# Layer norm's fp16 halves: the high half from one ScalarE instruction, the fp32 value and the low half on VectorE

## The reference

```
h = maximum(layernorm(x), 0);  x = x + attention(h, adj)     # 8 heads of 64, softmax over adj's edges
h = maximum(layernorm(x), 0);  x = x + relation(h, adj)      # rel = adj.T * (q k^T), each row divided by its norm; rel @ v
```

## Time and profile before

| what | value |
|---|---|
| median of 3 runs | 2466.06 us (2464.73 to 2466.9) |
| the profiled execution's own time | 2466.99 us |
| its span in the trace | 2465.2 us |
| TensorE busy, VectorE, ScalarE, GpSimd | 97%, 57%, 68%, 53% of the span |
| mean granted TensorE clock | 0.994 |

### The profile page before, as it was taken

The page is one execution under the profiler, slowest core; times in us unless marked ns, Lnnn a source line. Parts: engine busy times, 40 slices in busy tenths (PEclk is TensorE's granted clock), DMA queues, the critical chain, the costliest instruction groups (busy, mean ns, idle before and its releaser), DMA issues.

```text
span 2465.2 us, 53413 instructions
## 1 busy us (share of the span) xinstructions
PE 2396.9 (97%) x19252; PEld 1304.5 (53%) x19252; DVE 1411.2 (57%) x4432; ACT 1682.6 (68%) x4108; POOL 1296.1 (53%) x1159
## 2 busy tenths in 40 slices
PE   5899999999999999999999999999999999999986
PEld 2455555555555555555555555555555555555543
DVE  4555665555665555665555666555666555665543
ACT  4676766677766776766767766777766776766762
POOL 2555555555555555555555555555555555555541
PEclk9999999999999999999999999999999999999998
DMA  6566665775666666765666765666666666665642
GB/s 179 121 125 129 150 134 126 136 142 129 147 137 124 135 146 126 149 136 120 139 138 133 146 140 120 140 139 132 150 138 119 140 141 130 151 134 119 125 112 64
DMA packets 938792, 329.13 MB, mean 134 GB/s; under 512 B 885920, under 2 KB 886176, under 8 KB 938528
## 3 DMA queue, kind: packets, MB, share of 16 engines
q1 hardware_dynamic: 936272, 323.35, 63.1%
q10 hardware_dynamic: 2256, 2.36, 0.4%
HBM read 73.93 MB, written 33.55 MB: 44 GB/s over the span
## 4 chain that ended last, share of the span: by engine, by line
PE 89%; DMA 4%; ACT 3%; POOL 1%; DVE 1%; issue 1%; SPq 1%; DVEq 0%; ACTq 0%; POOLq 0%
PE B L677 75%; PE O L677 7%; PE S L751 7%; DMA probs_t<-halves 2%; DMA h0t<-h_halves 1%; ACT h L414 1%; ACT probs L474 1%; POOL h_halves L361 1%; PE B L707 1%; ACT h_halves L421 1%; POOL halves L375 1%; SPq L319 0%; POOL guess L356 0%; DMA h1t<-h_halves 0%; DVE masked L611 0%
## 5 line engine op out<-in xcount | busy, mean ns | idle before, releaser
L375 POOL TENSOR_TENSOR halves<-probs,halves 128x512 f16<-128x512 f32 x512 | 593.2, 1163 | 573.5 <-ACT halves L482 573.4
L474 ACT ACTIVATE probs<-masked,neg_max 128x256 f32<-128x256 f32 x1024 | 508.0, 497 | 229.6 <-DVE neg_max L611 229.5
L611 DVE CUSTOM_DVE_ANT_0 masked<-S,mask 128x256 f32<-128x256 f32 x1024 | 384.6, 418 | 126.4 <-PE S L751 126.3
L677 PE MATMUL B<-h0t,wq 128*128 128x512 f16 x1536 | 356.4, 382 | 32.2 <-DMA h0t<-h_halves 31.5
L361 POOL TENSOR_TENSOR h_halves<-h,h_halves 128x512 f16<-128x512 f32 x256 | 295.4, 1160 | 164.2 <-ACT h_halves L421 164.0
L677 PE MATMUL B<-wvt,h1t 128*128 128x512 f16 x1536 | 349.6, 381 | 9.8 <-DMA h1t<-h_halves 9.8
L677 PE MATMUL B<-h0t,wk 128*128 128x512 f16 x1536 | 352.8, 379 | 0.0
L677 PE MATMUL B<-wv,h0t 128*128 128x512 f16 x1536 | 352.2, 379 | 0.0
L677 PE MATMUL B<-h1t,wm 128*128 128x512 f16 x1536 | 346.9, 379 | 0.0
L482 ACT ACTIVATE halves<-probs 128x512 f16<-128x512 f32 x512 | 322.5, 630 | 16.2
L677 PEld LDWEIGHTS O<-v,probs_t 128*128 128x128 f16 x6144 | 248.3, 98 | 130.2 <-DMA probs_t<-halves 11.5
(11 more groups left out here) (70 smaller groups left out, 2894.7 us busy)
## 6 DMA issues: line engine op xcount, KB each, us to landing
x_in<-in_x_dram SPq DMA_DIRECT2D x128, 256.0 KB, 3.4
x_res<-in_x_dram SPq DMA_DIRECT2D x128, 256.0 KB, 3.7
out_dram<-result SPq DMA_DIRECT2D x128, 256.0 KB, 2.5
probs_t<-halves SPq DMA_TRANSPOSE x512, 2.8
h0t<-h_halves SPq DMA_TRANSPOSE x128, 3.2
h1t<-h_halves SPq DMA_TRANSPOSE x128, 3.3
rv<-in_L_gnn_Wq_dram SPq DMA_DIRECT2D x1, 1024.0 KB, 8.3
rq<-in_L_gnn_Wk_dram ACTq DMA_DIRECT2D x1, 1024.0 KB, 5.3
```

What stands on the lines that cost most here:

```text
L375: nc.gpsimd.tensor_tensor(halves[:, n % RING, 1, :], probs[:, n % 2, :, :].rearrange("p t n -> p (t n)"), halves[:, n % RING, 0, :], ALU.s ...
L474: ins = nc.scalar.activation(probs[:, n % 2, i, :], masked[:, n % 2, i, :], ACT.Exp, bias=neg_max[:, n % 2, i:i + 1], scale=-1.0, accum_ou ...
L611: ins = nc.vector.tensor_tensor_reduce(out=masked[:, n % 2, i, :], in0=S[n % 4][:, i, :], in1=mask[:, i, :], scale=SCORE, scalar=BIG, op0= ...
L677: ins = nc.tensor.matmul(dst, left(i), right(j), start=(n == 0), stop=(n == len(pairs) - 1))
```

## The change

In ln_apply's place ACT writes the fp16 high half directly, as relu(x * rstd + shift) rounded to fp16. DVE gets two instructions for each tile: `ln_apply`, a tensor_scalar that writes x * rstd + shift in fp32 to h (no ReLU), and `h_low_half`, a scalar_tensor_tensor that writes max(h, 0) minus the high half. POOL takes no part in either. A new step "low" in the plan says where DVE does the low half, and SP waits for and issues the transpose: for layer 1 within slot 12, for layer 0 in slots 18, 19, 22 and 25. The x loads now wait for the low half.

```diff
@@ BESIDE
-              12: [("ln1_scale", 0, 1), ("ln1_apply", 0, 1), ("ln1_split", 0, 1), ("ln1_apply", 1, 1),
-                   ("ln1_split", 1, 1), ("ln1_apply", 2, 1), ("ln1_split", 2, 1), ("ln1_apply", 3, 1),
-                   ("ln1_split", 3, 1), ("ln0_stats", 0, -1), ("ln0_stats", 1, -1)],
+              12: [("ln1_scale", 0, 1), ("ln1_apply", 0, 1), ("ln1_split", 0, 1), ("ln1_apply", 1, 1),
+                   ("ln1_split", 1, 1), ("ln1_low", 0, 1), ("ln1_apply", 2, 1), ("ln1_split", 2, 1),
+                   ("ln1_low", 1, 1), ("ln1_apply", 3, 1), ("ln1_split", 3, 1), ("ln1_low", 2, 1),
+                   ("ln0_stats", 0, -1), ("ln1_low", 3, 1), ("ln0_stats", 1, -1)],
...
-              18: [("ln0_apply", 0, -1), ("ln0_split", 0, -1), ("ln0_apply", 1, -1), ("ln0_split", 1, -1)],
+              18: [("ln0_apply", 0, -1), ("ln0_split", 0, -1), ("ln0_apply", 1, -1), ("ln0_split", 1, -1),
+                   ("ln0_low", 0, -1)],
+              19: [("ln0_low", 1, -1)],
               21: [("ln0_apply", 2, -1), ("ln0_split", 2, -1)],
+              22: [("ln0_low", 2, -1)],
               23: [("residual", 1, 0)],
-              24: [("ln0_apply", 3, -1), ("ln0_split", 3, -1)]}
+              24: [("ln0_apply", 3, -1), ("ln0_split", 3, -1)],
+              25: [("ln0_low", 3, -1)]}
@@ SP
-                    sp.wait_ge(ln_done[0], TILES * (p - 1) + n + 1)
+                    sp.wait_ge(h_low[0], TILES * (p - 1) + n + 1)
-                elif kind == "ln0_split" and p > 0:
+                elif kind == "ln0_low" and p > 0:
-                elif kind == "ln1_split":
+                elif kind == "ln1_low":
@@ POOL
-            def h_low_half(layer, n, pair):
-                pool.wait_ge(h_high[layer], TILES * pair + n + 1)
-                nc.gpsimd.tensor_tensor(h_halves[:, n, 1, :], h[:, n % 2, :],
-                                        h_halves[:, n, 0, :], ALU.subtract).then_inc(h_low[layer], 1)
@@ ACT
-                nc.scalar.activation(h[:, n % 2, :], src[:, n, :], ACT.Relu, scale=rstd[:, layer, n:n + 1],
-                                     bias=shift[:, layer, n:n + 1]).then_inc(ln_done[layer], 1)
-                nc.scalar.activation(h_halves[:, n, 0, :], h[:, n % 2, :],
-                                     ACT.Copy).then_inc(h_high[layer], 1)
+                nc.scalar.activation(h_halves[:, n, 0, :], src[:, n, :], ACT.Relu, scale=rstd[:, layer, n:n + 1],
+                                     bias=shift[:, layer, n:n + 1]).then_inc(h_high[layer], 1)
@@ DVE
+            def ln_apply(layer, src, n, pair, before, count):
+                dve.wait_ge(ln_scale[layer], pair + 1)
+                if n >= 2:
+                    dve.wait_ge(h_low[layer], TILES * pair + n - 1)
+                else:
+                    need(dve, before, count)
+                nc.vector.tensor_scalar(h[:, n % 2, :], src[:, n, :], rstd[:, layer, n:n + 1],
+                                        shift[:, layer, n:n + 1], ALU.mult, ALU.add).then_inc(ln_done[layer], 1)
+            def h_low_half(layer, n, pair):
+                dve.wait_ge(ln_done[layer], TILES * pair + n + 1)
+                dve.wait_ge(h_high[layer], TILES * pair + n + 1)
+                nc.vector.scalar_tensor_tensor(h_halves[:, n, 1, :], h[:, n % 2, :], 0.0, h_halves[:, n, 0, :],
+                                               ALU.max, ALU.subtract).then_inc(h_low[layer], 1)
```

More of the change, by code:

```diff
@@ L357, in ln_power @@
                                         ALU.pow).then_inc(ln_guess[layer], 1)
-            def h_low_half(layer, n, pair):
-                pool.wait_ge(h_high[layer], TILES * pair + n + 1)
-                nc.gpsimd.tensor_tensor(h_halves[:, n, 1, :], h[:, n % 2, :],
-                                        h_halves[:, n, 0, :], ALU.subtract).then_inc(h_low[layer], 1)
             ln_power(0, 1)
-            for n in range(TILES):
-                h_low_half(0, n, 0)
             for kind, n, p in pairs(PLAN):
@@ L381, in _ @@
                     ln_power(1, p + 1)
[L382 to L385, removed]
                 elif kind == "residual":
@@ L405, in _, with h_high_half @@
             act.dma_start(bv[:, :], bv0.partition_broadcast(P)).then_inc(small_loaded, 16)
-            def ln_apply(layer, src, n, pair, before, count):
+            def h_high_half(layer, src, n, pair, before, count):
                 act.wait_ge(ln_scale[layer], pair + 1)
[L410 to L413, removed]
-                nc.scalar.activation(h[:, n % 2, :], src[:, n, :], ACT.Relu, scale=rstd[:, layer, n:n + 1],
-                                     bias=shift[:, layer, n:n + 1]).then_inc(ln_done[layer], 1)
-            def h_high_half(layer, n, pair, before, count):
-                act.wait_ge(ln_done[layer], TILES * pair + n + 1)
                 need(act, before, count)
-                nc.scalar.activation(h_halves[:, n, 0, :], h[:, n % 2, :],
-                                     ACT.Copy).then_inc(h_high[layer], 1)
+                nc.scalar.activation(h_halves[:, n, 0, :], src[:, n, :], ACT.Relu, scale=rstd[:, layer, n:n + 1],
+                                     bias=shift[:, layer, n:n + 1]).then_inc(h_high[layer], 1)
             def weight_high(n, w, scale):
@@ L428, in _ @@
             for n in range(2):
-                ln_apply(0, x_in, n, 0, h_low[0], 0)
-            for n in range(2):
-                h_high_half(0, n, 0, h_turned[0][n], 0)
+                h_high_half(0, x_in, n, 0, h_turned[0][n], 0)
             act.dma_start(stage[1], wk0.rearrange("(t p) n -> p t n", p=P)).then_inc(w_loaded[1], 16)
@@ L434, in _ @@
             for n in range(2, 4):
-                ln_apply(0, x_in, n, 0, h_low[0], 0)
-            for n in range(2, 4):
-                h_high_half(0, n, 0, h_turned[0][n], 0)
+                h_high_half(0, x_in, n, 0, h_turned[0][n], 0)
             act.dma_start(stage[2], wv0.rearrange("(t p) n -> p t n", p=P)).then_inc(w_loaded[2], 16)
@@ L507, in _ @@
                     ins.then_inc(rel_high, 1)
-                elif kind == "ln0_apply" and p > 0:
-                    ln_apply(0, x_in, n, p, h_low[p > 1], TILES * max(p - 2, 0) + n + 3)
                 elif kind == "ln0_split" and p > 0:
-                    h_high_half(0, n, p, h_turned[p > 1][n], 16 * max(p - 1, 1))
-                elif kind == "ln1_apply":
-                    ln_apply(1, x_res[:, p % 2, :, :], n, p, h_low[0], TILES * min(p + 1, PAIRS - 1) + n + 3)
+                    h_high_half(0, x_in, n, p, h_turned[p > 1][n], 16 * max(p - 1, 1))
                 elif kind == "ln1_split":
-                    h_high_half(1, n, p, h_turned[0][n], 16 * min(p + 2, PAIRS))
+                    h_high_half(1, x_res[:, p % 2, :, :], n, p, h_turned[0][n], 16 * min(p + 2, PAIRS))
         @block.vector
@@ L563, in _ @@
             ln_scales(0, 1)
+            for n in range(2):
+                ln_apply(0, x_in, n, 0, h_low[0], 0)
+            for n in range(2):
+                h_low_half(0, n, 0)
             for n, (w, scale) in enumerate(((wq, QS), (wk, WS), (wv, WS))):
@@ L569, in _ @@
                                                ALU.mult, ALU.subtract).then_inc(w_low, 1)
+                if n == 0:
+                    for t in range(2, TILES):
+                        ln_apply(0, x_in, t, 0, h_low[0], 0)
+                    for t in range(2, TILES):
+                        h_low_half(0, t, 0)
             dve.wait_ge(small_loaded, 48)
@@ L660, in _ @@
                            rel_steps, 6 * p + 3 * n)
+                elif kind == "ln0_apply" and p > 0:
+                    ln_apply(0, x_in, n, p, h_low[p > 1], TILES * max(p - 2, 0) + n + 3)
+                elif kind == "ln0_low" and p > 0:
+                    h_low_half(0, n, p)
+                elif kind == "ln1_low":
+                    h_low_half(1, n, p)
+                elif kind == "ln1_apply":
+                    ln_apply(1, x_res[:, p % 2, :, :], n, p, h_low[0], TILES * min(p + 1, PAIRS - 1) + n + 3)
                 elif kind == "ln0_stats" and p > 0:
```

## The result

The changed kernel takes 2570.55 us (median of 4 runs, 2570.24 to 2570.9), the kernel before 2465.39 us in the same session. The ratio is 1.0431, 95% interval 1.0418 to 1.0443: slower by 105 us, about 3.3 us in each of the 32 turns. The forecast was 2564 us, slower.

What follows compares the result with a forecast made beforehand. TensorE, without idle time in the middle, was taken to bound the kernel. 63 us (Stall A) + 34 (Stall B) - 1 (ends) + 2 (jitter) = 98 us, from the median 2564 us; range 2528 to 2608.

Steps and rivals of the forecast that it cites:

- No idle time to win, every stall paid in full: Middle stretch: TensorE is busy 1119.06 of 1120 us, so whatever holds up a product adds to the end every turn.
- Stall A: Slots 12 to 16: DVE's longer queue delays q2's low half and so rv1, 2.08 us a turn, 63 us in all.
- the added work: Slot 12 on DVE: four applies, four low halves and their waits put the mask 4.41 us later.
- The two terms that give back: DVE ahead of q2's low half: 0.49 us from a shorter variance, 1.84 us of former waiting for ACT.
- Stall B: Slot 25: tile 3's low half stands behind k3's, so q0 waits for h0t, 1.1 us in 31 turns, 34 us.
- What the trace would show: TensorE idle about 100 us more: rv's product waiting 2 us for DVE, q0 waiting 1.1 us for DMA h0t.
- The rest at nothing: Other slots, x loads, POOL and the start: no cost, the start 0, give or take 1 us.
- The end: Last pair's h1t comes 0.4 + 0.8 us earlier without the copy and POOL's subtraction: -1.2 us.
- One stall alone: Rival: only the slot 12 stall is real, 2528 us, or only the slot 25 stall, 2499 us; chance 0.12.
- DVE and GpSimd hold each other up: Rival: added DVE instructions meet running POOL instructions, +140 us, 2704; at a third of that 2610 to 2620; chance 0.09.
- the rule: VectorE instructions with two SBUF inputs or 2-port mode and GpSimd instructions exclude each other; no such wait counted in slot 12.
- Not slower: Rival: DVE is late for nobody, no product waits and the ends' gain is left, 2465 us; chance 0.05.

Runs made afterwards that it cites:

- experiment 6: Changed kernel with layer 0's four bn_stats moved to slots 14 and 15, the scale to 17, tile 3's low half to 24: 2462.2 us, ratio 0.9995.
- experiment 7: experiment 6 with the low half of layer 0's tile 3 back in slot 25: 2496.1 us, ratio 1.0133.
- experiment 4: Kernel before the change with six additional bn_stats (3.6 us) on VectorE in slot 12: 2505.3 us, ratio 1.0163.
- experiment 5: Kernel before the change with two additional bn_stats (1.2 us) on VectorE in slot 12: 2464.9 us, ratio 1.0004.
- experiment 1: Changed kernel with the low half of layer 0's tile 3 moved from slot 25 to 24: 2533.5 us, ratio 1.0279.
- experiment 2: Changed kernel with apply, high and low half of layer 1's tiles 2 and 3 moved from slot 12 to 14 and 15: 2567.3 us, ratio 1.0413.
- experiment 3: Changed kernel with the edits of experiment 2 and experiment 1 together: 2528.6 us, ratio 1.0258.
- experiment 8: experiment 6 plus two bn_stats with one SBUF input each on DVE in slot 14: 2481.2 us, ratio 1.0071.
- experiment 9: experiment 6 plus two scalar_tensor_tensor with two SBUF inputs each on DVE in slot 14: 2509.9 us, ratio 1.0182.

## Why the prediction was right, point by point

- **No idle time to win, every stall paid in full.** Right. Experiments 6 and 7 show both sides: with the layer norm's load off ACT and POOL and no stall the time is the kernel before's, with one stall it is that stall times 31.
- **The total.** 2564 against 2570.55 is closer than the terms deserve. Stall A was 9 us too small, and 4.5 us that I hadn't foreseen at the start (below) went the other way. That part is luck.
- **Stall A, 2.08 us.** The mechanism and the place were right, 2.41 us the size. The term that was mis-sized is the added work, 4.75 instead of 4.41: the apply with two pointer operands takes 0.545 us (0.46 from start to start) where I took 0.48 and 0.40, which is 0.24 of the difference. Most of the rest is the wait ahead of applies 2 and 3, 0.18 to 0.19 us each where I took 0.11. The two terms that give back, 0.49 and 1.84, held; experiment 4 confirms their sum, experiment 5 that there is a threshold. 2.41 x 30 = 72 us against 63 forecast and 71 between experiments 1 and 6.
- **Stall B, 1.1 us.** Right: 1.07 in the timeline, 33.9 us over 31 turns in experiment 7 against 34. What the trace would show was wrong: I wrote that q0 would be seen waiting for the DMA, and the trace names rel in most turns.
- **The rest at nothing.** Right in the middle of the run, wrong at the start, where I had looked at the halves alone and not at the transfers that ACT issues behind them. ACT, freed of the copies and of their waits, issues the loads of wk and wv at 11.85 and 12.35 us; before it was 13.49 and 17.73 us. The profile after, ACT's queue:

```profile
11.85 0.37 ACTq L414 DMA_DIRECT2D rq<-in_L_gnn_Wk_dram  x1
...
12.35 0.43 ACTq L418 DMA_DIRECT2D x_res<-in_L_gnn_Wv_dram  x1
```

  The two loads of 1 MB are then out of the way sooner, the last h transpose of the first pair lands 3.20 us after its issue where it took 7.73, and TensorE's first product comes at 24.55 instead of 28.80 us. That the earlier loads are the cause is read from the order of these times, it wasn't tried. What speaks for the changed norm as the origin: the first product comes between 24.5 and 25.0 us in all eight kernels with the new layer norm and between 27.3 and 29.9 in the three with the old one. The end gave 1.1 us (1.2 forecast). The last product of the setup, in turn 0, ends at 82.95 us instead of 87.30, 4.4 us earlier. Together the two ends are -5.5 instead of -1, which partly makes up for the larger stall A: 72 + 33 - 5.5 = 99.5 of the 104 us between the two profiled executions. Of the other 4 us some 3 lie in single turns that take longer than the usual one (9 us of such excess against 6 before). In the longest wait of this kind q0 stands 2.38 us for a transpose that lands late:

```profile
1408.55 3.64 PE L685 MATMUL B<-h0t,wq 128*128 128x512 f16 x9 [2.38 <-DMA h0t<-h_halves]
```

- **The rivals.** One stall alone: no, both are real. DVE and GpSimd hold each other up: not in slot 12, as reckoned, but DVE was held in experiments 2 and 3, and the rule was written in the prediction before I moved the wrong work there. Not slower: no. DVE's instructions would have had to cost half.

## What to carry to other kernels

When one engine is busy without a gap, look for the hand-offs that it takes with no margin, and count for each edit what now stands ahead of them on the engine that makes them; taking 438 us off two other engines was worth nothing in the middle of this run and some 5 us at its ends. The list of waits shows such a place before it costs anything, as a weight load that was held for 0.3 us in each turn. When work has to be moved, look also at what kind of instruction it is, what GpSimd does in that slot, and which transfer waits for the result and what stands ahead of it in SP's queue. Four bn_stats, which GpSimd doesn't hold and no transfer waits for, went where two applies and two low halves could not, a difference of 66 us. The hold by itself is shown by experiments 8 and 9, where it cost 29 us.

## What the runs showed of the hardware

- A VectorE instruction with two SBUF inputs waits for a running GpSimd tensor_tensor to end (0.68 us became 1.53 in experiment 9), and so does a tensor_scalar from SBUF to SBUF in fp32 (0.545 us became 1.28 in experiment 3). A bn_stats with one SBUF input does not, nor does an instruction with one input in SBUF and one in PSUM (L596, 0.737 to 0.753 us). Tiny instructions are held as well: in experiment 6 a tensor_tensor on 4 elements took 1.18 us and the tensor_scalar on 4 elements behind it 1.08, GpSimd being busy from 1250.09 to 1253.6 with three instructions:

```profile
1251.33 1.18 DVE L502 TENSOR_TENSOR ln_work<-ln_work,guess 128x4 f32<-128x4 f32 x1
1252.54 1.08 DVE L504 TENSOR_SCALAR ln_work<-ln_work 128x4 f32<-128x4 f32 x1
```

  The Trainium skill, page "SBUF — State Buffer", section "Who interferes with whom", says the same of both kinds, and that one SBUF input outside the 2-port modes leaves VectorE free of GpSimd. Experiments 8 and 9 agree.
- Per-partition operands aren't free: the tensor_scalar on 128x512 fp32 takes 0.420 us with a constant and 0.545 with two per-partition operands. That the new one has two operations isn't the reason: the mask's tensor_scalar in the kernel before (L574) has two, with constants, and takes 0.420 as well.
- ACT's fp16 output costs next to nothing more or less: 0.80 us for relu(x * scale + bias) into fp16, 0.807 into fp32.
